# Graph work spread over other steps of a trip, and GpSimd's last gather behind its norm and power

## The chip, the cores and the metric

The kernel runs on one core of one Trainium2 chip, and the metric is the device time of one execution in microseconds (us). A core has five engines: TensorE (matmuls and transposes), VectorE, ScalarE, GpSimd, and SyncE (SP), which issues most DMAs. In the rows they are PE (PEld for its weight loads), DVE, ACT, POOL and SP.

## The reference, cut to what matters

```python
xn = layernorm(x)                                   # x: 12500 x 256
agg = segment_sum((xn @ w_gnn)[src] * edge_weight[:, None], dst, 12500)   # 200000 edges, dst sorted
x = x + relu(agg) + linear_attention(xn)            # 4 heads of 64, layer norms on k and v
h = layernorm(x)
for _ in range(30):
    h = h + 0.01 * tanh(h)
    h = h * sigmoid(h)
    h = layernorm(h, ln_w, ln_b)
    h = h @ W.T + b
out = x + h
```

The 30 iterations are done for each row by itself. The graph part needs, for a row, the normed rows of all nodes that have an edge into it.

## The kernel before

Rows are handled in 98 tiles of 128. A prelude (the first 0.53 ms or so) norms all rows and stores them, sums the attention's products, folds the attention into one matrix w_mix, and does the graph work of the first tiles. Then come five rounds. A round holds the h of 20 tiles (18 in the first) in five quads of four tiles (the last quad of the first round has two) and takes them through the 30 iterations. One step (slot) is one iteration of one quad; a trip is 15 steps, three iterations of all five quads; ten trips make a round. In the first four rounds the trips also carry the graph work and the x rows of the next rounds' tiles: two graph tiles, A and B, and two x tiles a trip. The last round has none.

All instructions of an engine run in the order in which they are written; semaphores order the engines against each other. For step n (slot s of trip t) the engines do, each in its own queue (`f_trip` of each engine):

- TensorE (from L1549): transposes of quad n+1 (TR, L1467, 8 instructions), 24 matmuls of quad n (MM, L1475), then, in some steps, matmuls and transposes into XB (L1395, L1389) and a burst of graph matmuls into AGG (L1381). The transposes of n+1 wait for v_low of n, and for the norms by ScalarE and by GpSimd.
- ScalarE (L862): copy of the transposes (v_high, L778), in some steps a copy of XB (L737), three norms of quad n+2 (two in the last round, L769), silu of quad n+4 (L764), tanh of quad n+5 (L754).
- VectorE (L1298): v_low of n+1 (`f_low`, L1230), then in some steps graph and x work, then the shift sh of n+3 (L1198, needs GpSimd's rs), the statistics st of n+4 (L1188, two instructions, need silu), h + 0.01 tanh(h) of n+5 (`f_sum`, L1213, writes T), and the variance ve of n+4 (`f_var`, L1193).
- GpSimd (L668): two or three gathers of edge rows (indirect DMAs, L611), in two steps a power for x (`x_rstd`, x_rs), one norm of quad n+2 (two in the last round, `f_norm`, L646), the power (variance to the -1/2) of quad n+3 (`f_rstd`, L579). In the last round it also makes the variance (L638).
- SP (L533): loads of a graph tile's edges, of x rows and uncovered rows, stores of the summed x rows.

The work that a trip carries besides has fixed steps, given by constants. A tile's one-hot matrix hot is made by VectorE: `g_scalars` (L1077, L1078) in step 0 for A and 8 for B, `g_hot` (the marking, L1086, and the weighting, L1089) in steps 1 and 9. Gathers of A are issued in steps 0 to 7 and of B in 8 to 14, in lots of 2 or 3 (`G_A`, `G_B`), and the bursts that read them come `MUL_LAG = 2` steps later. At A_TAIL = 10 and B_TAIL = 2 the sum is copied (`g_copy`, L1095), transposed, multiplied by the graph weights, and read three steps behind (`g_read`, L1101). An x tile starts at step 0 or 6 (X_AT): transposed, copied and multiplied one step later, summed after two (`x_sum`, L1166), its statistics after three (`x_stats`, `x_mean`, `x_var`, L1170, L1174, L1178), its power after four, its norm after five (`x_norm`, L1182). The normed x tile is the next round's h_next. A round's last five steps end with `f_end` (L1238), and there `f_sum` reads h_next, not a product.

Of the kernel before, what the change touches and what calls it, by code (L numbers as in the profile page):

```python
# [15 lines left out]
EPS = 1e-5  # L16
# [12 lines left out]
QT = 4  # L29
# [61 lines left out]
SCALARS_AT, HOT_AT = (0, 8), (1, 9)  # L91
A_TAIL, B_TAIL = 10, 2
# [59 lines left out]
X_AT = (0, 6)  # L152
# [50 lines left out]
def build(nc, x, src, dst, ew, src_laid, dst_laid, ew_laid, w_gnn, wq, wk_t, wv_t, wo_t, bo, gk, bk, gv, bv, ln_w, ln_b, wf_t, bf, out):  # L203
# [14 lines left out]
    with ctx:  # L218
# [103 lines left out]
        x_ve = sb("x_ve", [128, 1])  # L322
        x_rs = sb("x_rs", [128, 1])
# [19 lines left out]
        ve = [sb(f"ve{q}", [128, QT]) for q in range(QUADS)]  # L343
        rs = [sb(f"rs{q}", [128, QT]) for q in range(QUADS)]
# [217 lines left out]
        def _(pool):  # L562
# [67 lines left out]
            def x_rstd(i):  # L630
                rstd(x_rs[0:R], x_ve[0:R], 1, "x_variance", i + 1, "x_rstd")


            def f_rstd(n, q):
                tiles = unit_tiles(n)
                if n >= LAST_ROUND:
                    pool.wait_ge(S("stats"), n + 1)
                    pool.tensor_scalar(ve[q][0:R], st[q][0:R, :, 2], 1.0 / D, EPS, ALU.mult, ALU.add).then_inc(S("variance"), 1)  # L638
                rstd(rs[q][0:R, 0:tiles], ve[q][0:R, 0:tiles], tiles, "variance", n + 1, "rstd")
# [28 lines left out]
            def f_trip(t, h, r, u, end, g, xx, last):  # L668
                for s in range(SLOTS):
                    n = t * SLOTS + s  # L670
                    if g:
                        first_tile, second_tile = gathers_at(s)
                        for i in first_tile:
                            gather(t * 2 + EARLY_G, i, first_tile[-1] if i == first_tile[0] else None)
                        for i in second_tile:
                            gather(t * 2 + (EARLY_G + 1), i, second_tile[-1] if i == second_tile[0] else None)
# [12 lines left out]
        def _(act):  # L689
# [172 lines left out]
            def f_trip(t, h, r, u, end, g, xx, last):  # L862
                for s in range(SLOTS):
                    n = t * SLOTS + s
                    if not (last and s + 1 >= SLOTS):
                        copy_t(n + 1, (h + s + 1) % 2, n)
                    if xx and s == X_AT[0] + 1:
                        xb_copy(xb_use(t, 0), True)
                    if xx and s == B_TAIL + 2:
                        xb_copy(xb_use(t, 1), False)  # L870
                    if xx and s == X_AT[1] + 1:
                        xb_copy(xb_use(t, 2), True)
                    if g and s == A_TAIL + 2:
# [16 lines left out]
        def _(dve):  # L890
# [189 lines left out]
            def g_hot(j):  # L1080
# [5 lines left out]
                v.tensor_tensor(hot[e][:], by_pair(d_loc), iota_f[:].rearrange("p (j w) -> p j w", w=WIDE).unsqueeze(2).broadcast_to([128, SIDES, DEEP, WIDE]),  # L1086
                                ALU.is_equal).then_inc(S("hot_marked"), 1)
                dve.wait_ge(S("hot_marked"), j + 1)
                v.tensor_tensor(hot[e][:], hot[e][:], by_pair(w_loc), ALU.mult).then_inc(S("hot_ready"), 1)  # L1089
# [86 lines left out]
            def x_var(i):  # L1176
                dve.wait_ge(S("x_mean"), i + 1)
                v.tensor_scalar(x_ve[0:R], x_mv[0:R, 1:2], EPS, None, ALU.add).then_inc(S("x_variance"), 1)  # L1178

            def x_norm(i, at):  # L1180
                dve.wait_ge(S("x_rstd"), i + 1)
                v.tensor_scalar(h_next[0:R, bass.ds(at, 1), :].rearrange("p t f -> p (t f)"), x_1[0:R], x_mv[0:R, 0:1], x_rs[0:R, 0:1],  # L1182
# [63 lines left out]
            for s in range(EARLY_STEPS):  # L1246
# [12 lines left out]
                for j, i in early_chunks(s + 1, EARLY_G * KC):  # L1259
                    if i == 0:  # L1260
                        g_scalars(j)
                        g_hot(j)
# [35 lines left out]
            def f_trip(t, h, r, u, end, g, xx, last):  # L1298
                for s in range(SLOTS):
# [5 lines left out]
                    if g:  # L1305
                        for e in range(2):
                            if s == SCALARS_AT[e]:
                                g_scalars(t * 2 + (EARLY_G + e))
                            if s == HOT_AT[e]:
                                g_hot(t * 2 + (EARLY_G + e))  # L1310
                    if xx and s == B_TAIL:
                        g_copy(t * 2 + (EARLY_G - 1))
                    if g and s == A_TAIL:
                        g_copy(t * 2 + EARLY_G)
                    if xx and s == B_TAIL + 3:
                        g_read(t * 2 + (EARLY_G - 1), xb_use(t, 1), g_x[0:R], g_out[1][0:R])
                    if g and s == A_TAIL + 3:
                        g_read(t * 2 + EARLY_G, xb_use(t, 3), g_x[0:R], g_out[0][0:R])
                    if xx:
                        for e in range(2):  # L1320
                            if s == X_AT[e] + 2:
                                x_sum(t * 2 + e, e, xb_use(t, 2 * e))
                            if s == X_AT[e] + 3:
                                x_stats(t * 2 + e)
                                x_mean(t * 2 + e)
                                x_var(t * 2 + e)
                            if s == X_AT[e] + 5:
                                x_norm(t * 2 + e, u * 2 + e)
# [11 lines left out]
                    if not (last and s + 4 >= SLOTS):  # L1340
                        f_var(n + 4, (s + 4) % QUADS)
# [5 lines left out]
        def _(pe):  # L1347
# [201 lines left out]
            def f_trip(t, h, r, u, end, g, xx, last):  # L1549
                for s in range(SLOTS):  # L1550
# [5 lines left out]
                    if xx:  # L1556
                        if s == X_AT[0] + 1:
                            xb_multiply(w_mix, xb_use(t, 0))
                        if s == B_TAIL + 2:
                            xb_multiply(w_agg, xb_use(t, 1))  # L1560
                        if s == X_AT[1] + 1:
                            xb_multiply(w_mix, xb_use(t, 2))
                        if s == X_AT[0]:
                            x_transpose(t * 2, "g_done", t * 2 + (EARLY_G - 1))
                        if s == B_TAIL + 1:
                            g_transpose(t * 2 + (EARLY_G - 1), "x_summed", t * 2 + 1)
                        if s == X_AT[1]:
# [3 lines left out]
                    if g:  # L1571
                        if s == A_TAIL + 2:
                            xb_multiply(w_agg, xb_use(t, 3))
                        if s == A_TAIL + 1:
# [42 lines left out]
```

## Time and profile before

| | us |
|---|---|
| median of 3 runs | 4040.45 |
| lowest and highest | 4038.16, 4040.65 |
| the profiled execution's own time | 4040.07 |
| its span, first to last instruction | 4038.3 |
| TensorE busy in the span | 3638.4 |

The profile is of one execution. Busy time is the time in which an engine has an instruction in work; the idle time of a group is put down to what ended it. The chain of waits is followed back from the last instruction, at each step to what released it. "issue" is time in which an engine waited for nothing that the profile shows, such as the preparation of a gather.

### The profile page before, as it was taken

The page shows a single profiled execution, that of the slowest core. Times are in us where ns is not written, and L with a number is a line of the kernel's source. Part 1 is how long each engine was busy: PE and PEld are TensorE (multiplying, and loading weights), DVE is VectorE, ACT ScalarE, POOL GpSimd, SP SyncE. Part 2 cuts the span into 40 slices and gives each one's busy share as a digit, 9 for nine tenths or more (in the row PEclk, how much of TensorE's full clock was granted, in tenths as well). Part 3 has the DMA queues.
Part 4 walks back from the last instruction along what each step waited for, and adds up shares of the span by engine and source line. Part 5 has one row for each costly group of instructions (what it writes and reads, how often), then busy time and mean ns, then how long its engine had stood idle before and what let it go on. Part 6 is the DMA issues. An engine that isn't in the chain of part 4 may idle for free.

```text
span 4038.3 us, 82503 instructions
## 1 busy us (share of the span) xinstructions
PE 3638.4 (90%) x30416; PEld 3235.8 (80%) x30416; DVE 3491.0 (86%) x6074; ACT 3356.6 (83%) x4895; POOL 3100.7 (77%) x3591
## 2 busy tenths in 40 slices
PE   0788868999899999999999999989999999999999
PEld 0565557888788888888888888888888888999999
DVE  6777668888888889888988888888988888999998
ACT  3333268888888899999898999989999999999998
POOL 5677788888888888888888888888888885555555
PEclk9999889999999999999999999999999999999999
DMA  8555332222223222232322222233222221100000
GB/s 292 170 160 151 112 89 80 81 80 81 82 79 101 84 83 79 80 86 76 108 84 81 79 84 84 78 91 96 77 82 85 78 83 47 53 1 1 1 1 27
DMA packets 215581, 340.29 MB, mean 84 GB/s; under 512 B 79352, under 2 KB 152694, under 8 KB 215186
## 3 DMA queue, kind: packets, MB, share of 16 engines
q0 software_dynamic: 80960, 219.99, 19.0%
q1 hardware_dynamic: 120126, 83.28, 7.1%
q10 hardware_dynamic: 14100, 31.75, 2.3%
q8 instruction: 249, 4.08, 0.4%
q14 instruction: 146, 1.20, 0.1%
HBM read 298.20 MB, written 36.65 MB: 83 GB/s over the span
## 4 chain that ended last, share of the span: by engine, by line
PE 36%; DVE 21%; POOL 20%; ACT 14%; issue 7%; DMA 1%; ACTq 0%; DVEq 0%; SPq 0%; POOLq 0%
PE MM L1475 17%; POOL gat_even L611 10%; PE TR L1467 10%; DVE st L1188 6%; ACT T L769 5%; POOL rs L579 5%; DVE v_low L1230 5%; ACT v_high L778 4%; PE AGG L1381 4%; ACT T L764 4%; DVE T L1213 3%; POOL T L646 2%; PE XB L1395 2%; POOL gat_odd L611 2%; PE MM L1427 2%
## 5 line engine op out<-in xcount | busy, mean ns | idle before, releaser
L611 POOL DMA_INDIRECT gat_even<-xn_d,src_cur x1496 | 1502.4, 1004 | 397.6 <-issue 387.3
L1475 PE MATMUL MM<-w_high,v_high 128*128 128x256 f32 x5880 | 1725.4, 293 | 0.0
L1475 PE MATMUL MM<-w_low,v_high 128*128 128x256 f32 x5880 | 1661.0, 282 | 0.0
L1475 PE MATMUL MM<-w_high,v_low 128*128 128x256 f32 x5880 | 1659.7, 282 | 0.0
L1188 DVE BATCH_NORM_STATS2 st<-T 128x6 f32<-128x512 f32 x1470 | 970.8, 701 | 181.4 <-ACT T L764 172.1
L1475 PEld LDWEIGHTS MM<-w_high,v_high 128*128 128x128 f32 x5880 | 1126.9, 192 | 0.0
L1475 PEld LDWEIGHTS MM<-w_low,v_high 128*128 128x128 f32 x5880 | 1125.6, 191 | 0.0
L1475 PEld LDWEIGHTS MM<-w_high,v_low 128*128 128x128 f32 x5880 | 1123.6, 191 | 0.0
L769 ACT ACTIVATE T<-T,sh,rs 128x256 f32<-128x256 f32 x2072 | 1095.3, 593 | 19.9 <-DVE sh L1198 19.9
L1467 PE MATMUL TR<-ident,T 128*128 128x128 f32 x5916 | 814.1, 281 | 207.8 <-DVE v_low L1230 154.2
L1467 PEld LDWEIGHTS TR<-ident,T 128*128 128x128 f32 x5916 | 649.3, 142 | 401.2 <-DVE v_low L1230 254.5
L778 ACT ACTIVATE v_high<-TR 128x1024 fp32r<-128x1024 f32 (+1 forms) x750 | 756.0, 1008 | 246.7 <-PE TR L1467 244.5
L1230 DVE SCALAR_TENSOR_TENSOR v_low<-TR,v_high 128x1024 fp32r<-128x1024 f32 (+1 forms) x750 | 896.9, 1196 | 30.7 <-ACT v_high L778 30.4
L579 POOL TENSOR_TENSOR rs<-ve,minus_half 128x4 f32<-128x4 f32 (+1 forms) x755 | 799.3, 1059 | 154.5 <-DVE ve L1193 135.2
L1213 DVE SCALAR_TENSOR_TENSOR T<-T,MM 128x1024 f32<-128x1024 f32 (+1 forms) x725 | 857.3, 1182 | 3.4 <-ACT T L754 3.4
L764 ACT ACTIVATE T<-T 128x1024 f32<-128x1024 f32 (+1 forms) x750 | 773.5, 1031 | 39.0 <-DVE T L1213 38.9
L754 ACT ACTIVATE T<-MM 128x1024 f32<-128x1024 f32 (+1 forms) x725 | 719.1, 992 | 10.3 <-PE MM L1475 10.0
L646 POOL TENSOR_SCALAR T<-T,rs,sh 128x256 f32<-128x256 f32 x868 | 508.4, 589 | 189.8 <-DVE sh L1198 167.3
L1381 PE MATMUL AGG<-gat_even,hot 128*32 128x256 f32 x4048 | 304.0, 391 | 24.1 <-DMA gat_even<-xn_d,src_cur 24.1
L1198 DVE SCALAR_TENSOR_TENSOR sh<-st,rs 128x4 f32<-128x4 f32 (+1 forms) x755 | 120.0, 159 | 165.0 <-POOL rs L579 160.4
L611 POOL DMA_INDIRECT gat_odd<-xn_d,src_cur x170 | 167.7, 986 | 51.2 <-issue 49.7
L1381 PEld LDWEIGHTS AGG<-gat_even,hot 128*32 128x32 f32 x4048 | 100.6, 109 | 132.3 <-issue 58.1
(201 smaller groups left out, 2454.1 us busy)
## 6 DMA issues: line engine op xcount, KB each, us to landing
gat_even<-xn_d,src_cur POOLq DMA_INDIRECT x1496
a_x<-in_x SPq DMA_DIRECT2D x24, 512.0 KB, 6.7
xn_d<-a_x ACTq DMA_DIRECT2D x24, 512.0 KB, 4.3
out_rows<-x_cur SPq DMA_DIRECT2D x23, 512.0 KB
a_x<-xn_d ACTq DMA_DIRECT2D x20, 512.0 KB, 3.7
x_n<-xn_d SPq DMA_DIRECT2D x80, 128.0 KB
x_d<-x SPq DMA_DIRECT2D x80, 128.0 KB
x_cur<-x_d SPq DMA_DIRECT2D x20, 512.0 KB, 4.5
```

What stands on the lines that cost most here:

```text
L579: pool.tensor_tensor(out_, var, minus_half[0:p, 0:n], ALU.pow).then_inc(S(done), 1)
L611: pool.indirect_dma_start(gat[gathered_in(j)][c][:], None, xn_d, bass.IndirectOffsetOnAxis(ap=src_cur[j % 2][:, c:c + 1], axis=0)).then_in ...
L646: last = pool.tensor_scalar(T[0:R, q * QT + t, :], T[0:R, q * QT + t, :], rs[q][0:R, t:t + 1], sh[q][0:R, t:t + 1], ALU.mult, ALU.add)
L754: nc.scalar.activation(lane(T, q, unit_tiles(n)), product(b, unit_tiles(n)), ACT.Tanh).then_inc(S("tanh_done"), 1)
L764: nc.scalar.activation(lane(T, q, unit_tiles(n)), lane(T, q, unit_tiles(n)), ACT.Silu).then_inc(S("silu_done"), 1)
L769: last = nc.scalar.activation(T[0:R, q * QT + t, :], T[0:R, q * QT + t, :], ACT.Identity, bias=sh[q][0:R, t:t + 1], scale=rs[q][0:R, t:t + 1])
L778: nc.scalar.activation(v_high[b][:, 0:banks], TR[:, 0:banks, 0:4 * R], ACT.Copy, bias=1.0).then_inc(S("transposed_copied"), 1)
L1188: last = v.bn_stats(st[q][0:R, t:t + 2].rearrange("p t k -> p (t k)"), rows_[:, t:t + 2, :].rearrange("p t f -> p f t"))
L1213: v.scalar_tensor_tensor(out=out_, in0=out_, scalar=0.01, in1=h, op0=ALU.mult, op1=ALU.add).then_inc(S("u_done"), 1)
L1230: v.scalar_tensor_tensor(out=v_low[b][:, 0:banks], in0=TR[:, 0:banks, 0:4 * R], scalar=1.0, in1=v_high[b][:, 0:banks], op0=ALU.add, op1=AL ...
L1467: last = tp(TR[:, t // 2, at:at + R], T[0:R, q * QT + t, h * 128:(h + 1) * 128], ident[0:R, 0:R])
L1475: last = mm(MM[b][0:R, t // 2, t % 2 * D:(t % 2 + 1) * D], rows_, w, start=k == 0, stop=k == len(products) - 1)
```

## The change

- `g_hot` is cut in two: `g_mark` (the marking) runs in steps 0 and 8, `g_hot` (the weighting) stays in 1 and 9. The B tile's `g_scalars` moves from step 8 to 5.
- The B tail's transpose, copy, multiply, read go from steps 3, 4, 4, 5 to 4, 5, 6, 7. The A tail's stay at 11, 12, 12, 13.
- The second x tile is transposed, copied, multiplied, summed in 8, 9, 9, 10 (was 6, 7, 7, 8), the statistics of the two x tiles come in 4 and 12 (were 3 and 9), their norms in 6 and 14 (were 5 and 11).
- The x tile's own power is gone: VectorE writes its variance into one more column of ve of the quad whose power comes next, and GpSimd's power of that quad has one element more.
- In GpSimd's queue the last gather of each step comes after that step's norm and power.
- In VectorE's queue `f_var` comes right behind `f_stats`, ahead of `f_sum`. Within a step `g_scalars`, `g_mark` and `g_hot` come behind the other work rather than ahead of it.

```diff
-SCALARS_AT, HOT_AT = (0, 8), (1, 9)
-A_TAIL, B_TAIL = 10, 2
+SCALARS_AT, MARK_AT, HOT_AT = (0, 5), (0, 8), (1, 9)
+A_SUMMED, B_SUMMED = 10, 2
+A_TAIL, B_TAIL = (11, 12, 12, 13), (4, 5, 6, 7)
...
-X_AT = (0, 6)
+X_AT = ((0, 1, 1, 2), (8, 9, 9, 10))
+X_STATS_AT, X_NORM_AT = (4, 12), (6, 14)
...
-        ve = [sb(f"ve{q}", [128, QT]) for q in range(QUADS)]
-        rs = [sb(f"rs{q}", [128, QT]) for q in range(QUADS)]
+        ve = [sb(f"ve{q}", [128, QT + 1]) for q in range(QUADS)]
+        rs = [sb(f"rs{q}", [128, QT + 1]) for q in range(QUADS)]
...
-            def f_rstd(n, q):
+            def f_rstd(n, q, x=None):
                 tiles = unit_tiles(n)
...
-                rstd(rs[q][0:R, 0:tiles], ve[q][0:R, 0:tiles], tiles, "variance", n + 1, "rstd")
+                if x is not None:
+                    pool.wait_ge(S("x_variance"), x + 1)
+                wide = tiles + (x is not None)
+                rstd(rs[q][0:R, 0:wide], ve[q][0:R, 0:wide], wide, "variance", n + 1, "rstd")
...
+                    def gathers(part):
+                        first_tile, second_tile = gathers_at(s)
+                        for i in first_tile[part]:
...
                     if g:
-                        first_tile, second_tile = gathers_at(s)
-                        for i in first_tile:
...
-                    for e in range(2):
-                        if xx and s == X_AT[e] + 4:
-                            x_rstd(t * 2 + e)
+                        gathers(slice(0, -1))
                     if not (last and s + 2 >= SLOTS):
                         f_norm(n + 2, (s + 2) % QUADS, BY_POOL[xx])
                     if not (last and s + 3 >= SLOTS):
-                        f_rstd(n + 3, (s + 3) % QUADS)
+                        f_rstd(n + 3, (s + 3) % QUADS, t * 2 + X_STATS_AT.index(s - 1) if xx and s - 1 in X_STATS_AT else None)
+                    if g:
+                        gathers(slice(-1, None))
...
-            def x_norm(i, at):
-                dve.wait_ge(S("x_rstd"), i + 1)
+            def x_norm(i, at, n, q):
+                dve.wait_ge(S("rstd"), n + 1)
...
                     if not (last and s + 4 >= SLOTS):
                         f_stats(n + 4, (s + 4) % QUADS)
+                        f_var(n + 4, (s + 4) % QUADS)
...
                     else:
                         f_sum(n + QUADS, q, product(b, unit_tiles(n)))
-                    if not (last and s + 4 >= SLOTS):
-                        f_var(n + 4, (s + 4) % QUADS)
```

## Rows read from the trace of the kernel before

**Rows 1.** The page: busy us of each engine over the whole span.

```profile
PE 3638.4 (90%) x30416; PEld 3235.8 (80%) x30416; DVE 3491.0 (86%) x6074; ACT 3356.6 (83%) x4895; POOL 3100.7 (77%) x3591
```

**Rows 2.** Line L1230 in 540:1220, 1240:3390, 3480:4015: ns min/median/max, first and last start.

```profile
L1230 DVE SCALAR_TENSOR_TENSOR v_low<-TR,v_high x141: 672/1215/1228, 564.8 to 1215.9; 128x1024 fp32r<-128x1024 f32 x113, 128x512 fp32r<-128x512 f32 x28
...
L1230 DVE SCALAR_TENSOR_TENSOR v_low<-TR,v_high x442: 678/1216/1236, 1243.7 to 3387.3; 128x1024 fp32r<-128x1024 f32 x147, 128x512 fp32r<-128x512 f32 x1
...
L1230 DVE SCALAR_TENSOR_TENSOR v_low<-TR,v_high x138: 1205/1217/1236, 3478.8 to 4013.9; 128x1024 fp32r<-128x1024 f32 x138
```

**Rows 3.** TensorE's transposes by group, in 1240:3390 and in 540:1220: busy, mean ns | idle.

```profile
L1467 PE MATMUL TR<-ident,T 128*128 128x128 f32 x3534 | 484.0, 281 | 120.2 <-DVE v_low L1230 112.7 <-POOL T L646 5.1
...
L1467 PE MATMUL TR<-ident,T 128*128 128x128 f32 x1024 | 145.4, 284 | 71.0 <-DVE v_low L1230 33.6 <-POOL T L646 30.6 <-ACT T L769 6.7
```

**Rows 4.** The chain of waits, steps 9 and 10 of a trip: start, us, what.

```profile
2117.01 0.88 DVE hot L1086
...
2117.91 0.96 DVE hot L1089
2118.87 0.35 DVE x_st L1170
...
2119.24 0.19 DVE x_mv L1174
...
2119.46 0.15 DVE x_ve L1178
...
2119.68 1.24 DVE st L1188 x2
...
2122.12 1.14 DVE v_low L1230
```

**Rows 5.** The timeline of TensorE at step 11 and at step 3 of the next trip.

```profile
2123.30 1.09 PE L1467 MATMUL TR<-ident,T 128*128 128x128 f32 x8 [2.31 <-DVE v_low L1230]
...
2157.54 1.09 PE L1467 MATMUL TR<-ident,T 128*128 128x128 f32 x8 [0.46 <-DVE v_low L1230]
```

**Rows 6.** GpSimd's groups by form in 1240:3390: busy us, mean ns | idle before.

```profile
L611 POOL DMA_INDIRECT gat_even<-xn_d,src_cur x998 | 1005.0, 1007 | 255.4 <-issue 255.4
L579 POOL TENSOR_TENSOR rs<-ve,minus_half 128x4 f32<-128x4 f32 x442 | 478.9, 1084 | 91.4 <-DVE ve L1193 86.0
L646 POOL TENSOR_SCALAR T<-T,rs,sh 128x256 f32<-128x256 f32 x442 | 269.3, 609 | 18.8 <-DVE sh L1198 0.9
```

**Rows 7.** Lines L579 and L646 in 1240:3390: ns min/median/max.

```profile
L579 POOL TENSOR_TENSOR rs<-ve,minus_half x443: 791/1038/1767, 1239.9 to 3387.5; 128x4 f32<-128x4 f32 x148
L579 POOL TENSOR_TENSOR x_rs<-x_ve,minus_half x59: 582/586/597, 1244.2 to 3356.8; 128x1 f32<-128x1 f32 x59
...
L646 POOL TENSOR_SCALAR T<-T,rs,sh x442: 544/553/1572, 1244.8 to 3388.8; 128x256 f32<-128x256 f32 x148
```

**Rows 8.** GpSimd's groups by form in 540:1220.

```profile
L611 POOL DMA_INDIRECT gat_even<-xn_d,src_cur x319 | 320.8, 1006 | 81.6 <-issue 81.6
L579 POOL TENSOR_TENSOR rs<-ve,minus_half 128x4 f32<-128x4 f32 x115 | 125.3, 1090 | 26.1 <-DVE ve L1193 24.9
```

**Rows 9.** Who waited for whom in 1240:3390: us in total, times, longest.

```profile
DVE st L1188 <- ACT T L764: 117.7, 182, 1.4
...
DVE sh L1198 <- POOL rs L579: 95.2, 123, 1.5
```

**Rows 10.** The timeline of GpSimd and VectorE where hot is made, two trips.

```profile
2151.96 1.77 POOL L579 TENSOR_TENSOR rs<-ve,minus_half 128x4 f32<-128x4 f32 x1
...
2151.79 1.02 DVE L1086 TENSOR_TENSOR hot<-d_loc,iota_f 128x768 f32<-128x768 f32 x1
...
2190.40 1.11 POOL L611 DMA_INDIRECT gat_even<-xn_d,src_cur  x1 [0.20 <-issue]
...
2190.62 0.96 DVE L1089 TENSOR_TENSOR hot<-hot,w_loc 128x768 f32<-128x768 f32 x1
```

**Rows 11.** VectorE's groups by form in 1240:3390: f_sum of a round's last five steps.

```profile
L1213 DVE SCALAR_TENSOR_TENSOR T<-T,h_next 128x1024 f32<-128x1024 f32 x15 | 18.6, 1241 | 0.0
```

More of the change, by code:

```diff
@@ L670, in f_trip @@
                     n = t * SLOTS + s
-                    if g:
-                        first_tile, second_tile = gathers_at(s)
-                        for i in first_tile:
-                            gather(t * 2 + EARLY_G, i, first_tile[-1] if i == first_tile[0] else None)
-                        for i in second_tile:
-                            gather(t * 2 + (EARLY_G + 1), i, second_tile[-1] if i == second_tile[0] else None)
-                    for e in range(2):
-                        if xx and s == X_AT[e] + 4:
-                            x_rstd(t * 2 + e)
+                    def gathers(part):
+                        first_tile, second_tile = gathers_at(s)
+                        for i in first_tile[part]:
+                            gather(t * 2 + EARLY_G, i, first_tile[-1] if i == first_tile[0] else None)
+                        for i in second_tile[part]:
+                            gather(t * 2 + (EARLY_G + 1), i, second_tile[-1] if i == second_tile[0] else None)
+                    if g:
+                        gathers(slice(0, -1))
                     if not (last and s + 2 >= SLOTS):
@@ L1087, in g_hot @@
                                 ALU.is_equal).then_inc(S("hot_marked"), 1)
+            def g_hot(j):
+                e = j % 2
                 dve.wait_ge(S("hot_marked"), j + 1)
@@ L1174, in x_mean, with x_var @@
                 v.bn_aggr(x_mv[0:R], x_st[0:R]).then_inc(S("x_mean"), 1)
-            def x_var(i):
+            def x_var(i, n, q):
                 dve.wait_ge(S("x_mean"), i + 1)
-                v.tensor_scalar(x_ve[0:R], x_mv[0:R, 1:2], EPS, None, ALU.add).then_inc(S("x_variance"), 1)
-            def x_norm(i, at):
-                dve.wait_ge(S("x_rstd"), i + 1)
-                v.tensor_scalar(h_next[0:R, bass.ds(at, 1), :].rearrange("p t f -> p (t f)"), x_1[0:R], x_mv[0:R, 0:1], x_rs[0:R, 0:1],
+                at = unit_tiles(n)
+                v.tensor_scalar(ve[q][0:R, at:at + 1], x_mv[0:R, 1:2], EPS, None, ALU.add).then_inc(S("x_variance"), 1)
+            def x_norm(i, at, n, q):
+                dve.wait_ge(S("rstd"), n + 1)
+                by = unit_tiles(n)
+                v.tensor_scalar(h_next[0:R, bass.ds(at, 1), :].rearrange("p t f -> p (t f)"), x_1[0:R], x_mv[0:R, 0:1], rs[q][0:R, by:by + 1],
                                 ALU.subtract, ALU.mult).then_inc(S("x_normed"), 1)
@@ L1261, in _ @@
                         g_scalars(j)
+                        g_mark(j)
                         g_hot(j)
@@ L1304, in f_trip @@
                         f_low(n + 1, 1 - b)
[L1305 to L1311, printed above, removed]
+                    if xx and s == B_SUMMED:
                         g_copy(t * 2 + (EARLY_G - 1))
-                    if g and s == A_TAIL:
+                    if g and s == A_SUMMED:
@@ L1314, in f_trip @@
                         g_copy(t * 2 + EARLY_G)
-                    if xx and s == B_TAIL + 3:
+                    if xx and s == B_TAIL[3]:
                         g_read(t * 2 + (EARLY_G - 1), xb_use(t, 1), g_x[0:R], g_out[1][0:R])
-                    if g and s == A_TAIL + 3:
+                    if g and s == A_TAIL[3]:
                         g_read(t * 2 + EARLY_G, xb_use(t, 3), g_x[0:R], g_out[0][0:R])
[L1319 to L1328, printed above, removed]
+                    for e in range(2):
+                        if xx and s == X_AT[e][3]:
+                            x_sum(t * 2 + e, e, xb_use(t, 2 * e))
+                        if xx and s == X_STATS_AT[e]:
+                            x_stats(t * 2 + e)
+                            x_mean(t * 2 + e)
+                            x_var(t * 2 + e, n + 4, (s + 4) % QUADS)
+                        if xx and s == X_NORM_AT[e]:
+                            x_norm(t * 2 + e, u * 2 + e, n + 2, (s + 2) % QUADS)
+                        if g and s == SCALARS_AT[e]:
+                            g_scalars(t * 2 + (EARLY_G + e))
+                        if g and s == MARK_AT[e]:
+                            g_mark(t * 2 + (EARLY_G + e))
+                        if g and s == HOT_AT[e]:
+                            g_hot(t * 2 + (EARLY_G + e))
```

32 lines of the change are left out of this document (14 added, 18 removed).

## The prediction

> **What bounds the kernel now.** I first read the busy shares: TensorE is busy for 90% of the span, but VectorE, ScalarE and GpSimd stand at 77 to 86% [rows 1]. No engine is far ahead, so a share says little; the question is where TensorE is made to wait. The change lies in the trip loop, so next I took that loop's speed from the splitting step v_low, which VectorE does once a step: 141 starts over 651.1 us in the first round (4.65 us a step, 69.8 a trip of 15), 442 starts over 2143.6 us in rounds two to four (4.86, so 72.9 a trip), 138 over 535.1 us in the last round, which has no graph work (3.91, so 58.6) [rows 2]. The change touches the first four rounds only, 40 trips; the 0.95 us a step that rounds two to four pay over the last one is partly work and partly waiting.
>
> The split of the two: in rounds two to four TensorE sat idle before the transposes TR for 120.2 us, 112.7 of it until a v_low; over 442/15 = 29.5 trips that is 4.1 us a trip, so TensorE's own work is 72.9 - 4.1 = 68.8 us a trip [rows 2, 3]. That 4.1 is all there is to win while TensorE's work stays as it is. In the first round the idle time before TR is 71.0 us, but 30.6 of it is on GpSimd's T [rows 3].
>
> Where in a trip? The chain of waits of one trip (steps 8 to 11) shows it [rows 4]: behind the v_low of step 9 stand the two operations on hot (0.88 and 0.96 us), then the statistics of x (0.35, 0.19, 0.15 us), and only then the step's own sh, st and so on, until v_low of step 10 releases TensorE. TensorE had waited 2.31 us for it; at step 3 of another trip, behind the first pair of hot, it waited 0.46 us [rows 5]. The rest of a trip goes over TensorE's own matmuls. So the loss sits in the steps in which VectorE has most to do, above all step 9.
>
> GpSimd is the second thing to read. Its slots in rounds two to four: 34 gathers a trip at 1.007 us plus 0.256 of issue (42.9), 15 powers at 1.084 (16.3), 15 norms at 0.609 + 0.04 (9.7) [rows 6], two x powers at 0.59 (1.2) [rows 7]. Sum 70.1 us of 72.9. It too has under 3 us to spare, and 86.0/29.5 = 2.9 us a trip is what its power waits for ve [rows 6]. In the first round 34 x 1.262 + 12 x 1.090 + 3 x 0.791 + 12 x 0.65 + 1.2 = 67.4 of 69.8 [rows 8, 6, 7]; TensorE has fewer tiles there, so GpSimd is the bound of that round.
>
> **The change part by part**, in the first four rounds.
>
> (1) The marking of hot goes from steps 1 and 9 to 0 and 8, the statistics of the second x tile from step 9 to 12. From the stretch [rows 4] go 0.88 + 0.02 + 0.35 + 0.02 + 0.19 + 0.02 + 0.15, some 1.6 us. In step 8 the mark takes the place of the scalars (moved to 5) and of x_sum (moved to 10), and st often waits for ScalarE's silu (117.7 us in 182 waits [rows 9]), so there it costs about nothing; without that cover it costs its 0.88. At step 0 nothing makes room for it, and it delays st by about what it saves in step 1; I count zero for the first pair. The g_read (5 to 7), x_norm (5 to 6 and 11 to 14), and the first x statistics (3 to 4) are 0.3 to 0.75 us each and go into steps whose chain runs over TensorE: zero, covered by the 3.9 us that TensorE has in every step anyway [rows 2].
>
> (2) ve stands ahead of T (f_sum) instead of behind it. VectorE then waits for its own st: for such a pair, x_st to x_mv, there is a gap of 0.02 us and no overlap, where now st and T overlap [rows 4]. I charge 0.1 us a step, and it counts only where VectorE is the chain: once or twice a trip. The bounds are 0 and 1.5 us a trip (15 steps). The next to be late would be silu, by T's 0.25 us of delay. The Trainium skill, VectorE: DVE Perf Modes, section "The DRAIN you can't avoid", says that a semaphore between chained operations costs nothing extra; by that the term would be 0. No run here shows it yet; the 0.02 us gap is close.
>
> In return ve comes 1.1 us earlier, which is T's time. VectorE had waited for GpSimd's power 95.2 us in 123 waits [rows 9]; the power now has T and v_low, to hide behind, v_low alone being 1.14 us [rows 4]. On the first round's GpSimd chain that counts directly.
>
> (3) GpSimd's last gather goes behind norm and power. The number of gathers and issue gaps stays. What it delays: the last gather of each step by 0.55 + 1.04 us [rows 7], and its landing; the bursts read it two steps (9 us) later, so zero. Behind the waiting power now stands one gather that used to be done before it. As ve comes 1.1 us earlier and the power is reached 1.26 us earlier, the waits for ve stay about as they are; bounds: all 2.9 us a trip gone, or 2.9 more. The SP queue's loads of edges for a B tile come a step-end gather later and are wanted at step 5 instead of 8; they are issued around step 14, five steps ahead: zero. Its store of the second x sum and the A edges behind it move from step 8 to 10, wanted at the next trip's step 0: zero.
>
> (4) The x power (0.586 us, twice a trip) is folded into the power of a quad, which gets a fifth element. Elements cost (1.038 - 0.791)/2 = 0.12 us each [rows 7], so GpSimd saves 2 x 0.59 - 2 x 0.12 = 0.94 us a trip; bounds 0.6 and 1.2.
>
> (5) GpSimd's stretched operations. A power takes 1.038 us in the median but up to 1.767, a norm 0.553 but up to 1.572 [rows 7], and a stretched one lies beside hot [rows 10]. (1.084 - 1.038) + (0.609 - 0.553), times 15, is 1.5 us a trip. A gather beside hot takes 1.11 us [rows 10], a tenth over the mean of 1.007 [rows 6]. With norm and power a gather earlier, and hot cut in two, a gather should stand beside hot oftener. I credit a third, 0.5 us a trip; bounds: 1.5 back, or 1.5 more, since four separate operations on hot can each hit one.
> The Trainium skill, SBUF — State Buffer, section "SBUF: two separate sides", has this as an exclusive lock between GpSimd and a VectorE operation with two SBUF inputs; the trace agrees for power and norm. By that rule T<-T,h_next in the last five steps of a round (1.24 us, both inputs in SBUF [rows 11]) would now hold off the very power that ve has just released, up to 4 x 5 x 1.24 = 25 us on GpSimd in all; VectorE's own T and v_low hide it, so the sum by the rule is the same to a few us.
>
> **The sum.** Rounds two to four: 1.6 - 0.1 = 1.5 us a trip off the stretch behind step 9, times 30 = 45. That leaves trips of 71.4 us, over GpSimd's 70.1 - 0.94 - 0.5 = 68.7 and TensorE's 68.8. First round, by GpSimd: 0.94 + 0.5, less 0.2 for its waits, 1.2 times 10 = 12. Together 57. The profiled execution took 4040.07 us (span 4038.3) against a median of 4040.45, so both give 3983. Prelude and last round stay.
>
> **Rivals.**
> - More decoupling than counted (chance 0.13): ve early and power early also take the idle at steps 0, 2 and 3, and trips reach TensorE's 68.8 + 0.9. For: the 95.2 us of waits for the power and its slack of 1.1 us. Against: GpSimd would be at 99%. 3.2 x 30 + 2.3 x 10 = 119, so 3921.
> - GpSimd becomes the bound (0.22): it keeps its 2.9 us of waits for ve, the steps with three gathers (3 x 1.26 + 0.6 + 1.08 = 5.5 us) outlast TensorE's, and the trip is 70.1 - 0.94 + 2.9 = 72.1: 0.8 off 30 trips and 0.4 off ten, 28 us, 4012. For: [rows 6]; against: TensorE is idle where VectorE is loaded, not on GpSimd's T.
> - The waits only move (0.08): the mark makes steps 0 and 8 late by what steps 1 and 9 gain, so the change doesn't do what it says: st of step 8 waits behind the mark rather than silu. 4040 less some 4, 4036.
> - Slower (0.12): the four separated operations on hot each hold off a norm or power, which now stand where the hot operations run. The price is up to 0.7 us each (1.767 - 1.038) against 1.5 us a trip now: 4 x 0.7 - 1.5 = 1.3, and T's delay of silu adds 0.2. It decides once GpSimd with its waits for ve has over 72.9 us a trip: 70.1 - 0.94 + 1.3 + 2.9 = 73.4, with 0.2 from silu 0.7 lost in each of 30 trips, and about as much in each of the first ten: 28 us, 4068. For: [rows 10]; against: norms and powers move away from hot in time, by 1.26 us.
>
> **How the numbers follow.** The forecast itself has 0.45. A measurement of this kernel tells 0.2% (8 us) from no change. Faster is forecast, first and second rival: 0.80; same 0.08; slower 0.12. The range leaves out 0.2 above (the last two rivals) and holds the rest: up to 4030, 18 us over the second rival, and down to 3918, under the first; that is also where (3) and (5) at half of their good ends, 1.6 us more in each of 40 trips, would lead.
>
> **What would show it.** In the new profile: the period of v_low 4.76 us in rounds two to four and 4.57 in the first, unchanged in the last; idle before TR down from 4.1 to about 2.6 us a trip, and no 2.3 us wait at step 11; DVE's waits for rs nearly gone; a power of five elements of 1.16 us; powers and norms with means nearer to 1.04 and 0.55. It would be wrong if TR begins to wait for GpSimd's T, if ve's wait for st shows far more than 0.1 us, or if st waits longer for silu than 117.7 us did before [rows 9].

## The result and the profile after

The changed kernel took 3929.36 us (3928.34 to 3930.39, 4 runs) against 4040.55 (4038.16 to 4043.76, 4 runs): a ratio of 0.9724, 95% interval 0.9707 to 0.9741, or 111 us faster. That lies in the range, on the forecast's side, and nearly twice as far as the 57 us of the sum: it is the first rival (3921), not the forecast (3983). The profiled span is 3928.0 us.

Busy us of each engine, on the page of the changed kernel, to be read against [rows 1]:

```profile
PE 3649.0 (93%) x30416; PEld 3249.5 (83%) x30416; DVE 3527.0 (90%) x6074; ACT 3348.0 (85%) x4895; POOL 3062.0 (78%) x3511
```

TensorE does the same in nearly the same busy time (3638 and 3649 us); what has gone is the time between. VectorE is busy 36 us longer.

Line v_low of the changed kernel in 540:1220, 1220:3290 and 3380:3900, as in [rows 2] (ns min/median/max, first and last start):

```profile
L1237 DVE SCALAR_TENSOR_TENSOR v_low<-TR,v_high x145: 676/1217/1226, 563.7 to 1216.6; 128x1024 fp32r<-128x1024 f32 x116, 128x512 fp32r<-128x512 f32 x29
...
L1237 DVE SCALAR_TENSOR_TENSOR v_low<-TR,v_high x446: 679/1217/1225, 1220.7 to 3289.5; 128x1024 fp32r<-128x1024 f32 x149
...
L1237 DVE SCALAR_TENSOR_TENSOR v_low<-TR,v_high x134: 1204/1217/1234, 3380.3 to 3899.5; 128x1024 fp32r<-128x1024 f32 x134
```

A trip takes 15 x 652.9/144 = 68.0 us in the first round (69.8 before), 15 x 2068.8/445 = 69.7 in rounds two to four (72.9 before), and in the last round 58.6 as before. So rounds two to four gave about 3.1 us a trip, some 92 us in all, and the first 1.8 a trip, 18 us. (From the first v_low of a round to the first of the next, the three rounds went from 2180.6 to 2089.7 us and the first from 701.5 to 682.9.)

TensorE's transposes by group, in 1220:3290 and 540:1220, against [rows 3]:

```profile
L1473 PE MATMUL TR<-ident,T 128*128 128x128 f32 x3556 | 482.6, 279 | 29.2 <-DVE v_low L1237 28.5 <-POOL T L645 0.2
...
L1473 PE MATMUL TR<-ident,T 128*128 128x128 f32 x1052 | 146.6, 281 | 46.6 <-DVE v_low L1237 23.1 <-POOL T L645 13.3 <-ACT T L770 8.4
```

The idle time before TR fell from 120.2 to 29.2 us in rounds two to four: from 4.1 us a trip to 29.2/29.7 = 1.0. That is nearly the whole gain there, and the trip has come down on TensorE's own 68.8 us. A trip inside a round (windows view, 2223.8:2293.0) shows TensorE busy in all but 0.5 us:

```profile
2223.80:2293.00 69.20, 68.74 (x596) 61.97 (x596) 65.61 (x113) 65.86 (x95) 59.22 (x65) 1.00 0.31 89
```

The columns are the window, its length, busy us and count of PE, PEld, DVE, ACT and POOL, the granted clock of TensorE (1.00 is the upper of its two levels, 2.4 GHz), the DMA share and GB/s.

A part of the gain is that clock. Two trips of round two of the kernel before (windows view):

```profile
1556.70:1629.70 73.00, 68.70 (x591) 61.88 (x591) 64.46 (x114) 65.67 (x94) 61.08 (x67) 0.98 0.28 78
...
1702.40:1774.30 71.90, 68.89 (x604) 62.09 (x603) 64.22 (x113) 66.74 (x96) 59.30 (x66) 1.00 0.29 84
```

For a part of the first of them the clock was at the lower level (1.2 GHz). Of the second to ninth trips of rounds two to four, twelve were like it and took 72.9 us in the mean, the twelve at 1.00 took 72.1: 0.8 us for a trip. By the clock records of the traces TensorE had the lower level for 79 us of the first four rounds before and for 30 us in the changed kernel, there nearly all in the first round (26.6 us). As an estimate, 0.8 us for each trip that is touched (21 before, 8 now) makes some 10 of the 111 us. What brought the clock down was not tried.

GpSimd's groups by form in 1220:3290, against [rows 6], and the lines of the gather, the power and the norm (ns min/median/max), against [rows 7]:

```profile
L611 POOL DMA_INDIRECT gat_even<-xn_d,src_cur x1000 | 1036.5, 1037 | 253.3 <-issue 243.5 <-PE AGG L1387 7.3
L579 POOL TENSOR_TENSOR rs<-ve,minus_half 128x4 f32<-128x4 f32 x386 | 407.1, 1055 | 26.5 <-DVE ve L1200 20.2
L645 POOL TENSOR_SCALAR T<-T,rs,sh 128x256 f32<-128x256 f32 x445 | 256.1, 576 | 26.6 <-DVE sh L1205 6.1
L579 POOL TENSOR_TENSOR rs<-ve,minus_half 128x5 f32<-128x5 f32 x59 | 70.9, 1201 | 1.8 <-DVE ve L1200 1.8
...
L611 POOL DMA_INDIRECT gat_even<-xn_d,src_cur x1000: 945/961/1872, 1219.5 to 3268.4; - x167
...
L579 POOL TENSOR_TENSOR rs<-ve,minus_half x446: 713/1044/2017, 1221.0 to 3288.6; 128x4 f32<-128x4 f32 x149
...
L645 POOL TENSOR_SCALAR T<-T,rs,sh x445: 552/557/1609, 1220.5 to 3286.7; 128x256 f32<-128x256 f32 x149
```

Powers and norms are stretched less in the mean (1.055 and 0.576 against 1.084 and 0.609; the longest are longer), gathers more (1.037 against 1.007). The power's waits for ve went from 86.0 to 22.0 us, sh's waits for rs from 95.2 to 53.6, and st's for silu from 117.7 to 21.4 (groups and waits in the same stretch). All three waits are shorter; sh's for rs is the one that is left in some size.

### The profile page after: what moved, and what is told of

Same layout as the page of the kernel before. It is cut to its first block, busy times and chain, and to the rows that moved or that the text cites. A ratio compares the mean times of both kernels' runs of the same rounds, so it can differ in the third digit from the quotient of the medians.

```text
span 3928.0 us, 82503 instructions
## 1 busy us (share of the span) xinstructions
PE 3649.0 (93%) x30416; PEld 3249.5 (83%) x30416; DVE 3527.0 (90%) x6074; ACT 3348.0 (85%) x4895; POOL 3062.0 (78%) x3511
## 4 chain that ended last, share of the span: by engine, by line
PE 37%; POOL 25%; DVE 19%; ACT 11%; issue 6%; DMA 1%; ACTq 0%; POOLq 0%; DVEq 0%; SPq 0%
PE MM L1481 18%; POOL gat_even L611 14%; PE TR L1473 10%; DVE st L1195 7%; POOL rs L579 6%; DVE v_low L1237 4%; DVE T L1220 4%; ACT T L770 4%; PE AGG L1387 4%; ACT v_high L779 3%; ACT T L765 3%; POOL T L645 3%; PE MM L1433 2%; PE XB L1401 2%; POOL gat_odd L611 2%
## 5 line engine op out<-in xcount | busy, mean ns | idle before, releaser
L611 POOL DMA_INDIRECT gat_even<-xn_d,src_cur x1496 | 1539.5, 1029 | 393.8 <-issue 363.9
L1473 PE MATMUL TR<-ident,T 128*128 128x128 f32 x5916 | 804.2, 279 | 89.5 <-DVE v_low L1237 58.3
L579 POOL TENSOR_TENSOR rs<-ve,minus_half 128x4 f32<-128x4 f32 (+2 forms) x755 | 790.0, 1046 | 73.3 <-DVE ve L1200 52.4
L645 POOL TENSOR_SCALAR T<-T,rs,sh 128x256 f32<-128x256 f32 x868 | 491.7, 570 | 208.8 <-DVE sh L1205 182.8
```

The lines of the kernel that those rows point to most:

```text
L579: pool.tensor_tensor(out_, var, minus_half[0:p, 0:n], ALU.pow).then_inc(S(done), 1)
L611: pool.indirect_dma_start(gat[gathered_in(j)][c][:], None, xn_d, bass.IndirectOffsetOnAxis(ap=src_cur[j % 2][:, c:c + 1], axis=0)).then_in ...
L645: last = pool.tensor_scalar(T[0:R, q * QT + t, :], T[0:R, q * QT + t, :], rs[q][0:R, t:t + 1], sh[q][0:R, t:t + 1], ALU.mult, ALU.add)
L1473: last = tp(TR[:, t // 2, at:at + R], T[0:R, q * QT + t, h * 128:(h + 1) * 128], ident[0:R, 0:R])
```

## The experiments

Two theories stood after the result. The **spread theory** is the forecast's: heavy VectorE steps made TensorE wait, and moving work out of them paid. The **order theory**: VectorE and GpSimd waited for each other step by step, and the early ve and the late gather undid that. Four parts can be told apart: (a) the spread, (b) the last gather's place, (c) ve ahead of f_sum, (d) the folded x power. The order of the graph work within a step of VectorE stays new in all runs; in the changed kernel no step holds both an operation on the edges (scalars, marking, weighting) and x or tail work, so that order can only touch a_undone and x_back.

The first four kernels ran on another chip, on which the kernel before took 4173.4 us: there the stretch ahead of the loop is 90 to 97 us longer (the first v_low ends at 655 us, in b_undone at 663, against 566), and the loop of the kernel before, by what is left, some 40. So a difference of a few us between two of these four says nothing. They are compared with each other and, for (b) and (d), run again beside the changed kernel on a chip like the first.

**a_undone.** All but the spread.

```diff
-SCALARS_AT, MARK_AT, HOT_AT = (0, 5), (0, 8), (1, 9)
-A_TAIL, B_TAIL = (11, 12, 12, 13), (4, 5, 6, 7)
-X_AT = ((0, 1, 1, 2), (8, 9, 9, 10))
-X_STATS_AT, X_NORM_AT = (4, 12), (6, 14)
+SCALARS_AT, MARK_AT, HOT_AT = (0, 8), (1, 9), (1, 9)
+A_TAIL, B_TAIL = (11, 12, 12, 13), (3, 4, 4, 5)
+X_AT = ((0, 1, 1, 2), (6, 7, 7, 8))
+X_STATS_AT, X_NORM_AT = (3, 9), (5, 11)
```

> The changed kernel with the work of a trip put back at its old steps (marking 1 and 9, second x tile from step 6, statistics at 3 and 9), the new orders of VectorE's and GpSimd's queues kept. If the spread is what paid (spread theory: heavy steps 9 and 1 made TensorE wait), the 2.3 us wait at step 11 is back and it takes 3980 to 4000. If the early ve and the late gather paid (order theory: VectorE and GpSimd no longer wait on each other step by step), it takes 3935 to 3955.

Measured: 4168.1 us against 4173.4, ratio 0.9988 (0.9979 to 0.9998). Without the spread the rest is worth 5 us, less than either theory had said (3980 to 4000 would be a ratio of 0.985 to 0.990). In rounds two to four of its trace (1370:3550) the idle before TR is back, at 110.1/29.8 = 3.7 us a trip:

```profile
L1473 PE MATMUL TR<-ident,T 128*128 128x128 f32 x3574 | 487.3, 280 | 110.1 <-DVE v_low L1237 95.4 <-issue 8.8 <-ACT T L770 3.9
```

So far the runs say that next to nothing is won without the spread.

**a_only.** The spread alone: the edits of b_undone, c_undone and d_undone below, together.

> The kernel before with the spread alone: new steps, but all gathers first, ve behind f_sum, and the x tile's own power. Each of the new orders alone is worth little without the spread (with all but the spread the ratio was 0.9988). Spread theory: it has most of the gain alone, 60 to 75 us of 111. Order theory: spread and early ve pay only together, since TensorE's wait goes over VectorE's heavy steps and then over GpSimd's lag; 20 to 45 us.

Measured: 4008.42 us against 4041.93, ratio 0.9918 (0.9901 to 0.9934), 33.5 us of 112.6. So the spread alone isn't it either: 5 and 33.5 us apart, 112 together (the 5 us on the second chip). And of the 33.5 us some 14 are the clock's, by the same estimate: it was at the lower level in 3 trips here, for 10 us, against 21 trips and 79 us before. Its trace in 1250:3390 (PE's group, POOL's norm, and the waits):

```profile
L1479 PE MATMUL TR<-ident,T 128*128 128x128 f32 x3576 | 481.2, 278 | 115.7 <-DVE v_low L1242 78.9 <-POOL T L650 36.7
...
L650 POOL TENSOR_SCALAR T<-T,rs,sh 128x256 f32<-128x256 f32 x448 | 304.1, 679 | 21.9 <-DVE sh L1210 4.2
...
DVE sh L1210 <- POOL rs L581: 174.7, 144, 1.6
```

TensorE idles nearly as long as before, but the cause is in part another: it now waits 36.7 us for GpSimd's norm itself (5.1 before), VectorE's sh, which the next v_low stands behind, waits 174.7 us for the power (95.2 before), and the norm's mean has gone from 0.609 to 0.679 us. GpSimd is the late one.

**c_undone.** ve behind f_sum again.

```diff
                         f_stats(n + 4, (s + 4) % QUADS)
-                        f_var(n + 4, (s + 4) % QUADS)
...
                         f_sum(n + QUADS, q, product(b, unit_tiles(n)))
+                    if not (last and s + 4 >= SLOTS):
+                        f_var(n + 4, (s + 4) % QUADS)
```

> The changed kernel with the variance ve behind f_sum again. Spread theory: 0 to 5 us slower (VectorE saves 0.1 us a step, GpSimd's waits for ve grow): 3925 to 3935. Order theory: GpSimd reaches its power 1.26 us earlier and now waits 1.1 us longer for ve, with a gather behind it; GpSimd has under 1 us a trip to spare, so 3960 to 4010.

Measured: 4097.8 us on the second chip, ratio 0.9818 (0.9802 to 0.9834), which is 48.7 us over b_undone on the same chip (4049.11). By the loop alone, which leaves out the stretch ahead of it, it is 57 us (2846.6 against 2789.9 from the first v_low to the end of round four). The ratio, 3967 us on a chip like the first, lies in the order theory's range. VectorE of this kernel and GpSimd around a trip's first two operations on hot (timeline):

```profile
2359.76 0.96 DVE L1087 TENSOR_TENSOR hot<-d_loc,iota_f 128x768 f32<-128x768 f32 x1
...
2364.28 0.94 DVE L1094 TENSOR_TENSOR hot<-hot,w_loc 128x768 f32<-128x768 f32 x1
2366.66 0.16 DVE L1205 SCALAR_TENSOR_TENSOR sh<-st,rs 128x4 f32<-128x4 f32 x1 [1.43 <-POOL rs L579]
...
2360.03 1.64 POOL L611 DMA_INDIRECT gat_even<-xn_d,src_cur  x1 [0.20 <-issue]
...
2364.22 1.40 POOL L645 TENSOR_SCALAR T<-T,rs,sh 128x256 f32<-128x256 f32 x1
2365.55 1.07 POOL L579 TENSOR_TENSOR rs<-ve,minus_half 128x4 f32<-128x4 f32 x1
```

The same place in the changed kernel:

```profile
2228.37 0.98 DVE L1087 TENSOR_TENSOR hot<-d_loc,iota_f 128x768 f32<-128x768 f32 x1
...
2230.70 0.17 DVE L1200 TENSOR_SCALAR ve<-st 128x4 f32<-128x4 f32 x1
...
2233.05 0.94 DVE L1094 TENSOR_TENSOR hot<-hot,w_loc 128x768 f32<-128x768 f32 x1
2233.91 0.15 DVE L1205 SCALAR_TENSOR_TENSOR sh<-st,rs 128x4 f32<-128x4 f32 x1
...
2231.99 0.56 POOL L645 TENSOR_SCALAR T<-T,rs,sh 128x256 f32<-128x256 f32 x1
2232.51 1.05 POOL L579 TENSOR_TENSOR rs<-ve,minus_half 128x4 f32<-128x4 f32 x1
2233.76 1.17 POOL L611 DMA_INDIRECT gat_even<-xn_d,src_cur  x1 [0.20 <-issue]
```

In the kernel with ve late, a gather is held beside the marking (1.64 us), the norm is then reached just as the weighting of hot starts and takes 1.40 us, the power ends late, and sh stands for 1.43 us; the next v_low and TensorE come after it. With ve early the norm is over before the weighting starts and the power 0.5 us into it, sh doesn't wait, and only a gather (1.17 us) is held beside it. In 1345:3480 sh waits 166.7 us for rs, against 53.6, and the norm's mean is 0.684 us against 0.576.

This is no single case. Norms that ran beside a hot operation and took over 0.15 us more than the median, counted in the traces of rounds two to four: 57 in c_undone, longer by 47.0 us together, and 56 in a_only (46.1 us), the two kernels with the spread and ve late; 15 in the kernel before (11.6 us); none in the changed kernel, in b_undone or in a_undone. So the held norms come to about the price of (c). How a late ve brings the norm to just that place these lines don't show: no power in them waits for ve, and over the rounds those waits are only 53.0 us here, 41.4 in b_undone (1340:3430).

**b_undone** and **b_undone_2.** All gathers of a step first; the second run beside its control.

```diff
-                        gathers(slice(0, -1))
+                        gathers(slice(0, None))
...
-                    if g:
-                        gathers(slice(-1, None))
```

> The changed kernel with all gathers of a step ahead of the norm and the power again. Spread theory: GpSimd has 0.4 us of slack a trip and the place of one gather matters little, 3930 to 3940. Order theory: norms and powers come 1.26 us later and meet the hot operations again, 3950 to 3975, with waits of sh for rs back.

> The changed kernel with all gathers of a step ahead of norm and power, repeated beside its control. If the last gather's place matters by the 0.4 us a trip that the trace on the other chip shows (69.7 against 69.3): 8 to 20 us slower than the control, 3937 to 3950. If not, within 5 us of it.

Measured: 4049.11 us on the second chip, 0.9700 (0.9684 to 0.9716); then 3928.84 against 4043.17, 0.9719 (0.9706 to 0.9732), with the control at 3927.99. With ve early the place of the last gather is worth nothing: 0.9 us with ranges that overlap. The idle before TR in 1240:3315 is the changed kernel's:

```profile
L1471 PE MATMUL TR<-ident,T 128*128 128x128 f32 x3576 | 485.2, 279 | 28.4 <-DVE v_low L1235 27.9
```

Half of the order theory falls with this: it is the early ve, not the late gather. With ve late the gather's place was not tried by itself; there (b) and (d) together seem to be worth more, for c_undone, which has them, stands at 0.9818 and a_only, which lacks them, at 0.9918, on two chips.

**d_undone** and **d_undone_2.** The x tile's own power again.

```diff
+                    if xx and s - 1 in X_STATS_AT:
+                        x_rstd(t * 2 + X_STATS_AT.index(s - 1))
...
-                v.tensor_scalar(ve[q][0:R, at:at + 1], x_mv[0:R, 1:2], EPS, None, ALU.add).then_inc(S("x_variance"), 1)
+                v.tensor_scalar(x_ve[0:R], x_mv[0:R, 1:2], EPS, None, ALU.add).then_inc(S("x_variance"), 1)
```

> The changed kernel with the x tile's own power on GpSimd again, twice a trip, ahead of the norm. GpSimd then has 0.9 us more a trip, 69.7 us of work against TensorE's 69.2: if GpSimd is the next bound, 20 to 35 us slower (3950 to 3965); if its lag is absorbed elsewhere, under 10 us (3930 to 3939).

> The changed kernel with the x tile's own power again, repeated beside its control. If GpSimd is the next bound, its 0.9 us a trip come back nearly whole in 40 trips (70.2 us a trip on the other chip): 25 to 40 us slower than the control, 3955 to 3970. If GpSimd's lag is absorbed, within 10 us.

Measured: 4065.6 us on the second chip, 0.9739 (0.9723 to 0.9756); then 3939.19 against the control's 3927.99, ratio to the kernel before 0.9745 (0.9732 to 0.9758). So (d) is worth 11 us, just over the lower of the two expectations. The first rounds of the two traces (v_low of d_undone_2, then of the control):

```profile
L1244 DVE SCALAR_TENSOR_TENSOR v_low<-TR,v_high x151: 675/1217/1226, 565.0 to 1248.3; 128x1024 fp32r<-128x1024 f32 x121, 128x512 fp32r<-128x512 f32 x30
```

```profile
L1237 DVE SCALAR_TENSOR_TENSOR v_low<-TR,v_high x151: 676/1217/1226, 565.6 to 1248.8; 128x1024 fp32r<-128x1024 f32 x121, 128x512 fp32r<-128x512 f32 x30
```

683.3 and 683.2 us: in the first round, where I had booked the folded power, it gives nothing. The 11 us are in rounds two to four. On the second chip d_undone is 16.5 us over b_undone, and its first round 10.7 (698.5 against 687.8 us); the clock was at the lower level for 29.6 us of that round, against 9.2, so this isn't a price of the power alone. The 11 us may also be net of something else: in rounds two to four the median matmul into MM takes 281 ns in d_undone_2 and 283 in the changed kernel (weight loads 188 and 192), and TensorE is busy for 11.8 us less. Why was not tried.

**mark_back** and **x_back.** The two halves of the spread, each put back alone.

```diff
-SCALARS_AT, MARK_AT, HOT_AT = (0, 5), (0, 8), (1, 9)
+SCALARS_AT, MARK_AT, HOT_AT = (0, 5), (1, 9), (1, 9)
```

```diff
-A_TAIL, B_TAIL = (11, 12, 12, 13), (4, 5, 6, 7)
-X_AT = ((0, 1, 1, 2), (8, 9, 9, 10))
-X_STATS_AT, X_NORM_AT = (4, 12), (6, 14)
+A_TAIL, B_TAIL = (11, 12, 12, 13), (3, 4, 4, 5)
+X_AT = ((0, 1, 1, 2), (6, 7, 7, 8))
+X_STATS_AT, X_NORM_AT = (3, 9), (5, 11)
```

> The changed kernel with only the marking of hot back beside the weighting (steps 1 and 9). VectorE then has 3.8 + 1.85 = 5.65 us in steps 1 and 9, TensorE 5.3 in both. Spread theory, by step loads: 0.35 us twice a trip, 15 to 30 us slower than the changed kernel. If only the sum over a few steps counts (TensorE's own step 9 is now long): under 10 us.

> The changed kernel with only the x and B tail schedule back (second x tile from step 6, statistics at 3 and 9, norms at 5 and 11, tail of B 3 to 5). VectorE's step 9 is 3.8 + 0.96 + 0.75 = 5.5 us, TensorE's 4.6 and 3.95 behind it: by step loads 0.9 us a trip at step 11, 25 to 40 us slower than the changed kernel; if the mark alone is what the spread is worth, under 10 us.

Measured, beside after_again (3929.31): 3955.07 (0.9787, 0.9770 to 0.9803), 25.8 us slower, and 3973.7 (0.9834, 0.9817 to 0.9850), 44.4 us slower. TensorE's group in mark_back (1240:3340), then its wait at step 11 of one trip (timeline):

```profile
L1473 PE MATMUL TR<-ident,T 128*128 128x128 f32 x3568 | 482.8, 278 | 64.0 <-DVE v_low L1237 64.0
```

```profile
2212.61 1.09 PE L1473 MATMUL TR<-ident,T 128*128 128x128 f32 x8 [1.32 <-DVE v_low L1237]
```

The idle before TR is 64.0/29.7 = 2.2 us a trip, all of it until a v_low, and in x_back 70.9 us (1240:3360), 2.4 a trip. Either half alone leaves a VectorE stretch that outlasts TensorE's; both have to go. The load of single steps, which I had used for the expectation, named the first size (15 to 30) and was somewhat low for the second (25 to 40).

**after_again** and **after_third**, the controls, are the changed kernel itself.

> The changed kernel itself, as the control beside the next three and, by its ratio to the kernel before, for the four kernels that ran on another chip than the first measurement. Both theories: ratio 0.970 to 0.974 if the chips differ only ahead of the loop.

> The changed kernel once more as the control of this call. Both theories: ratio 0.972 to the kernel before on a chip where that takes 4041, and the loop's four rounds 2771 us; should this be the chip where the kernel before takes 4173, the ratio tells what the four earlier kernels there stand against: 0.968 to 0.972 if only the stretch ahead of the loop is slower.

Measured: 3929.31 against 4041.93 (0.9722, 0.9706 to 0.9738) and 3927.99 against 4043.17 (0.9717, 0.9704 to 0.9730). Neither landed on the slower chip, so how (a) and (c) stand there to the changed kernel itself was not measured; they are read against b_undone, which equals it on the other chip.

**marks_by_round.** mark_back's first round was shorter than the changed kernel's, its others longer, so the marks go back in the first round alone.

```diff
-                        if g and s == MARK_AT[e]:
+                        if g and s == (HOT_AT if r == 0 else MARK_AT)[e]:
```

> The changed kernel with the marking beside the weighting (steps 1 and 9) in the first round alone, and at 0 and 8 later. With the marks back in all rounds the first round took 673.7 us against 682.7 and the others 10.8 us longer each. If the rounds are independent: 9 us faster than the control, 3920. If the first round's gain was an accident of phase: within 3 us of the control.

Measured: 3921.43 us (3920.23 to 3922.53) against the control's 3927.99 (3926.64 to 3930.41); ratio to the kernel before 0.9701 (0.9688 to 0.9714). It beats both kernels, by 6.6 us the changed one. Its first round takes 673.3 us between first and last v_low, the control's 683.2. GpSimd's gathers in its first round (540:1200):

```profile
L611 POOL DMA_INDIRECT gat_even<-xn_d,src_cur x321 | 324.0, 1009 | 82.0 <-issue 80.8 <-PE AGG L1387 1.2
```

and in the control's:

```profile
L611 POOL DMA_INDIRECT gat_even<-xn_d,src_cur x316 | 326.4, 1033 | 79.7 <-issue 67.2 <-PE AGG L1387 9.1 <-DVE ve L1200 2.7
```

Two operations on hot a few us apart hold its gathers longer than a pair does: 24 ns a gather over 340 gathers is 8 us. But the two-element powers of that round give most of it back (0.93 us each against 0.72, thirty of them), and GpSimd is busy only 2.4 us less. The granted clock (windows view, the first round of marks_by_round, then of the control) says more:

```profile
563.90:1237.20 673.30, 634.02 (x5488) 564.45 (x5480) 612.33 (x1089) 610.07 (x908) 563.63 (x610) 1.00 0.30 85
```

```profile
565.60:1248.80 683.20, 647.14 (x5488) 578.13 (x5480) 609.05 (x1088) 610.04 (x908) 566.07 (x610) 0.98 0.29 84
```

TensorE does the same work in 13.1 us less busy time, with the clock at the lower level for 1.1 us against 30.7. The changed kernel's own profile has both kinds of trip in its first round: 68.1 us where the clock fell, 67.4 at 1.00; marks_by_round's take 67.1. So some 0.8 of the 1.1 us a trip go with the clock. Why it stays up with the marks beside the weightings was not tried.

## Why the prediction was right, and where its size was off

**What bounds the kernel.** Right: TensorE's own 68.8 us a trip stayed, the 4.1 us of idle time before TR was nearly all that could be won, and the changed kernel won 3.1 of it. The reading left out the granted clock: half of the trips of rounds two to four had some of it at the lower level and took 72.9 us, not 72.1, and the sum has no term for the estimated 10 us that its rise gave.

**(1) The spread.** The stretch behind step 9 was right, and so was its sign: a_undone brings nearly all the waits back. "I count zero for the first pair" was too low: the wait at step 3 (0.46 us in [rows 5], 1.0 in the mean of round three) is gone from the changed kernel and comes back, at 0.5, with mark_back, which costs 25.8 us in all. And the gain of the stretch was booked as the 1.5 us by which it got shorter, though TensorE had stood 2.31 us there and stands not at all now.

**(2) The early ve.** This is the step that failed. I booked it as a cost (0.1 us) in rounds two to four and as a help only to the first round. The runs turn it round. It is worth 48.7 us once the rest is in, since the spread alone turns a part of TensorE's wait for VectorE into a wait for GpSimd (a_only: sh waits 174.7 us for rs, TensorE 36.7 us for the norm). The sum looked at one engine's stretch at a time and compared trip totals, 68.7 for GpSimd against 71.4; a total doesn't show that a late norm meets the operation on hot (57 norms lengthened in rounds two to four of c_undone, none in the changed kernel). Its cost was fair: ve now starts 1.35 us after st (2229.35 to 2230.70), where T started 1.24 after it [rows 4]. The Trainium skill, VectorE: DVE Perf Modes, section "The DRAIN you can't avoid", would have this cost at 0; the trace shows 0.11 us of lost overlap, and no run here takes its effect on the time apart from the gain.

**(3) The last gather.** Zero was right, for itself and for its cover: b_undone_2 differs by 0.9 us. The waits for ve did not stay "about as they are": they fell from 86.0 to 22.0 us. That is not the early ve alone: with the spread and a late ve (a_only, 1250:3390) they are 37.0 us, with an early ve and no spread (a_undone) 115.6.

**(4) The folded power.** 1.20 us for five elements against my 1.16, so 2 x 0.59 - 2 x 0.16 = 0.86 us a trip off GpSimd. Its effect was booked in the wrong round: 0 in the first, 11 us in the other three. Whether "GpSimd is the bound of that round" holds for the changed kernel stays open: with the x powers back (d_undone_2) the round takes as long, but GpSimd is busy for only 2.6 us more in it (568.6 against 566.1), since its gathers took 1.014 us in place of 1.036.

**(5) Stretched operations.** I credited a third of 1.5 us. Norm and power together now give (1.055 - 1.038) + (0.576 - 0.553), times 15, or 0.6 us: 0.9 us came back, but 34 gathers pay 1.0 for it. A gather beside hot was put at "a tenth over the mean" from a row in which the gather had started first [rows 10]; c_undone shows 1.64 us. The page SBUF — State Buffer of the Trainium skill, section "SBUF: two separate sides", tells of an exclusive lock held for the whole instruction, and these rows agree for gathers too. Which of two operations starts first decided less sharply here than that page has it: the norm at 2364.22 started 0.06 us ahead of the weighting and was held all the same. On T<-T,h_next, where the prediction used that rule: in the last steps of a round of the changed kernel a norm beside it takes 1.42 and 1.61 us (at 1926.80 and 1931.82 in the timeline of GpSimd). So it was mostly the norm that was held; a power was held twice in rounds two to four, for 2.01 and 2.02 us (at 1948.72 and 2646.59), and VectorE's operation itself took up to 1.67 us against a median of 1.22. The last trips of the first three rounds are 3 to 4 us longer than the others, as they were before; no run takes apart why.

**The rivals.** The first came true, with its for: sh's waits for rs and the slack that the early ve gives; its against, GpSimd at 99%, was no obstacle. GpSimd as the late engine is what a_only shows, at 4008 where I had put 4012: the rival was right about a kernel that has the spread alone, and the nearness of the two numbers is luck, for some 14 us of that gain are the clock's. "The waits only move" and "slower" did not occur: the norms moved away from hot, as their against said. Chances of 0.13 for the first and 0.45 for the forecast were too far apart, for both rested on the same rows.

## What to carry to other kernels

When several engines of an in-order pipeline each have a few per cent to spare, comparing their totals is not enough. Follow one hand-over between two of them through a heavy step, and see which operation it makes late next; two edits that give 5 and 33 us alone can give 112 together, so undo each from the full change rather than try each alone. Read the granted clock beside every such difference: here it carried some 14 of one run's 33.5 us and most of another's 6.6. A small result that another engine waits for should be issued ahead of longer work whose result is wanted later: it cost 0.1 us of overlap a step here and gave 49 us in all. And operations of VectorE and GpSimd that hold each other off (here hot with norm or gather) are priced by what stands beside them, which a change of phase changes.

## What the runs showed of the hardware

A power on GpSimd costs 0.586 us for one element a partition, 0.71 for two, 1.04 for four, 1.20 for five. Beside an operation of VectorE with two SBUF inputs (hot, 0.95 us, or T<-T,h_next, 1.22 us) a norm of 0.56 us took up to 1.61, a power of 1.04 up to 2.02 and an indirect gather of 0.96 us up to 1.87. The folding of a small operation saved less than its length where it joined the engine's longest one: 0.43 us of 0.59. A trip of some 70 us in which TensorE's granted clock fell to its lower level for a part took 0.6 to 0.9 us longer, in the mean of a kernel's trips, than those at the upper one (the second chip left out). And one chip gave the kernel before 4173 us where the others gave 4041 to 4043, 90 us of it ahead of the loop; why wasn't looked into.
